# Streamed second attention: queries earlier and outputs later on TensorE, value halves first on ScalarE and VectorE, one turned load a store earlier

## The reference

```python
def _L1_xattn_ref(text_hidden, vision_tokens, vision_mask, Wq, Wk, Wv, Wo):
    q = (text_hidden @ Wq).reshape(B, T_text, N_HEADS, HEAD_DIM).transpose(0, 2, 1, 3)
    k = (vision_tokens @ Wk).reshape(B, T_vis, N_KV_HEADS, HEAD_DIM).transpose(0, 2, 1, 3)
    v = (vision_tokens @ Wv).reshape(B, T_vis, N_KV_HEADS, HEAD_DIM).transpose(0, 2, 1, 3)
    k = jnp.repeat(k, GROUPS, axis=1)
    v = jnp.repeat(v, GROUPS, axis=1)
    scores = jnp.einsum('bhtd,bhsd->bhts', q, k) / scale
    scores = jnp.where(mask, scores, -jnp.inf)
    attn = jax.nn.softmax(scores, axis=-1)
    out = jnp.einsum('bhts,bhsd->bhtd', attn, v)
    return out.transpose(0, 2, 1, 3).reshape(B, T_text, N_HEADS * HEAD_DIM) @ Wo
...
x = x + _L1_xattn_ref(_layernorm(x, axis=-1), ctx_1024, mask_BxS2_bf1, L1_xattn_Wq, L1_xattn_Wk, L1_xattn_Wv, L1_xattn_Wo)
```

## Time and profile before

| | |
|---|---|
| median of 3 runs | 2336.04 us |
| the profiled execution's own time | 2327.82 us |
| its span | 2326.0 us, mean granted clock 0.971 |
| PE busy | 2193.5 us (94%), 10153 matmuls |
| DVE, ACT, POOL busy | 1459.6 (63%), 1043.2 (45%), 771.1 us (33%) |
| streamed units | from about 885 to 1684 us |

### The profile page before, as it was taken

How to read it: one execution, slowest core, us unless ns; L and a number is a source line. 1 busy time by engine, 2 the same in 40 slices (tenths; PEclk the granted TensorE clock), 3 DMA queues, 4 the chain that set the end, 5 groups by cost and what they waited for, 6 DMA issues and landing times. The chain is left out here.

```text
span 2326.0 us, 32392 instructions
## 1 busy us (share of the span) xinstructions
PE 2193.5 (94%) x10153; PEld 1786.1 (77%) x10153; DVE 1459.6 (63%) x2989; ACT 1043.2 (45%) x1895; POOL 771.1 (33%) x705
## 2 busy tenths in 40 slices
PE   8999999999999997888888889888899999999999
PEld 6778788889999875666666666666677888888887
DVE  7755366647777676666666666666667555564544
ACT  5532211015565565556555556555555332332321
POOL 4423555511111443444444444444421302121000
PEclk9999999999999999999999999999999999999999
DMA  6423221127777766555555555555501223232331
GB/s 220 150 81 100 59 46 32 32 79 280 283 266 269 284 217 205 178 171 182 174 182 171 176 180 176 176 173 175 168 24 67 83 96 113 82 127 82 109 113 50
DMA packets 250573, 339.17 MB, mean 146 GB/s; under 512 B 22048, under 2 KB 159776, under 8 KB 247648
## 3 DMA queue, kind: packets, MB, share of 16 engines
q1 hardware_dynamic: 242224, 310.75, 40.7%
q0 software_dynamic: 8240, 27.01, 4.5%
HBM read 234.12 MB, written 103.55 MB: 145 GB/s over the span
## 5 line engine op out<-in xcount | busy, mean ns | idle before, releaser
L2269 POOL TENSOR_TENSOR xa_late_hi<-late_rows,route_wv_hi 128x512 fp32r<-128x512 f32 x228 | 290.3, 1295 | 389.5 <-ACT route_wv_hi L2336 388.6
L2362 ACT ACTIVATE route_weights<-route_weights,xa_minus_max 128x512 f32<-128x512 f32 x256 | 185.3, 724 | 360.8 <-DVE xa_minus_max L2562 360.7
L90 PE MATMUL xa_ps_o<-route_first_lo,xa_late_lo 128*128 128x512 f32 x256 | 114.3, 447 | 73.7 <-DVE xa_late_lo L2553 73.7
L2562 DVE CUSTOM_DVE_ANT_0 route_weights<-xa_ps_s,route_mask_bias 128x512 f32<-128x512 f32 x252 | 172.6, 685 | 9.8 <-issue 8.5
L2643 DVE STREAM_TRANSPOSE route_weights<-route_weights 128x512 f32<-128x512 f32 x228 | 160.0, 702 | 9.9 <-DMA xa_pt<-route_weights 7.4
L3305 ACT ACTIVATE ffn_silu<-ffn_ps_gate,late_scales 128x512 f32<-128x512 f32 x63 | 43.4, 688 | 247.3 <-PE ffn_ps_gate L92 247.3
L2584 DVE TENSOR_TENSOR x<-xa_ps_o,x 128x512 f32<-128x512 f32 x126 | 86.2, 684 | 92.1 <-PE xa_ps_o L92 92.0
L2336 ACT ACTIVATE route_wv_hi<-late_rows 128x512 fp32r<-128x512 f32 x228 | 129.6, 617 | 0.4 <-DMA late_rows<-xa_pt 0.4
L90 PEld LDWEIGHTS xa_ps_o<-route_first_lo,xa_late_lo 128*128 128x128 f32 x256 | 52.5, 205 | 96.4 <-issue 77.5
L90 PE MATMUL xa_ps_s<-route_kv_hi,xa_q_hi 128*128 128x512 f32 x256 | 110.8, 433 | 16.5 <-DVE xa_q_lo L2553 9.0
L1539 POOL DMA_INDIRECT route_rows<-moe_xn,route_slot_token x39 | 44.5, 1140 | 240.1 <-PE ex_ps_t L1832 182.5
(11 more groups left out here) (585 smaller groups left out, 6767.5 us busy)
## 6 DMA issues: line engine op xcount, KB each, us to landing
xa_pt<-route_weights SPq DMA_DIRECT2D x228, 256.0 KB, 2.0
late_rows<-xa_pt SPq DMA_DIRECT2D x456, 128.0 KB, 2.7
route_weights<-in_ffn_w SPq DMA_DIRECT2D x64, 512.0 KB, 3.7
route_weights<-in_expert_w SPq DMA_DIRECT2D x12, 1408.0 KB, 6.3
route_weights<-wd_folded SPq DMA_DIRECT2D x64, 256.0 KB, 2.6
ex_w_raw<-in_expert_w SPq DMA_DIRECT2D x10, 1408.0 KB, 6.3
moe_y<-ex_y SPq DMA_DIRECT2D x39, 256.0 KB, 3.6
route_weights<-in_expert_w SPq DMA_DIRECT2D x12, 768.0 KB, 8.9
```

The source lines that it names most:

```text
L90: pe.matmul(out, lh, rh, start=start, stop=False)
L2269: pool.tensor_tensor(lo, raw_part(half, two), f32(hi), ALU.subtract).then_inc(M.pt_ready, PART)
L2362: act.activation(prob[slot][:], prob[slot][:], ACT.Exp, bias=nmx[:, slot:slot + 1], scale=-1.0, accum_out=tot[:, slot:slot + 1]).then_inc( ...
L2562: dve.tensor_tensor_reduce(out=prob[slot][:], in0=psS[slot % 2][:], in1=mask_of(b, quarters), scale=-SCALE, scalar=3.4e38, op0=ALU.add, op ...
```

## The change

No operation is added, removed or resized. Four lists are put in another order. On PE the queries come right behind scores 3 and scores 0, the outputs behind scores 1 and scores 2. On ACT the value product's high half and the first turned half stand ahead of the first exponential, the second turned half behind it, the query's high half behind the exponential of tile 0, and the key or value copy later. On DVE the value product's low half comes right behind turn 0, the query's low half behind turn 3, and the additions to `x` around the last maximum. On SP the second half of a unit's turned tile is loaded behind its own store 3 instead of behind the next unit's store 0, and POOL makes all four low parts ahead of the key or value part. The order of waits moves with the operations.

```diff
--- before.py
+++ after.py
@@ -2216,21 +2216,19 @@
                     for ul, b, h, pair, u, i, left in units(g, which):
                         if which == "last" and ul > 0:
                             return
-                        before, again = features(g, which, ul, u)
 
                         def store(tt):
                             sp.wait_ge(M.blocks_turned, i + tt + 1)
                             sp.dma_start(G.pt_dram[ul % 2, tt], blocked[tt % 2][:]).then_inc(pt_stored[tt % 2], 16)
 
                         store(0)
-                        if before:
-                            load_turned((ul - 1) % 2, u - 1, 1)
                         store(1)
                         store(2)
                         if which == "first" and u == 0:
                             sp.wait_ge(R.xn_turned, NT)
                         load_turned(ul % 2, u, 0)
                         store(3)
+                        load_turned(ul % 2, u, 1)
                         if h == 1:
                             next_kv(pair + 1, g, b + 1)
                         if ul == 3:
@@ -2240,7 +2238,6 @@
 
                 groups(sp, body)
                 END = (GROUPS - 1) * UNITS + 1
-                load_turned(0, END - 1, 1)
                 load_gate_up(sp, io, G, L, 0)
                 load_down(sp, G, L, 0)
                 next_kv((GROUPS - 1) * B + 1, GROUPS - 1, 1)
@@ -2293,15 +2290,12 @@
                             break
                         before, _ = features(g, which, ul, u)
                         if before:
-                            turned_low(u - 1, 0, 0)
-                            turned_low(u - 1, 0, 1)
+                            for part in range(4):
+                                turned_low(u - 1, part // 2, part % 2)
                         if h == 0:
                             key_low(pair + 1, (b + 1) % B)
                         else:
                             kv_low(pair + 1, (b + 1) % B)
-                        if before:
-                            turned_low(u - 1, 1, 0)
-                            turned_low(u - 1, 1, 1)
                     if which != "last":
                         return
                     for part in range(4):
@@ -2419,24 +2413,24 @@
                         if which == "last" and ul > 0:
                             return
                         before, has_pv = features(g, which, ul, u)
-                        exp(i + 3, 3)
                         if has_pv:
                             proj_high(streamed_pv(u - 2), o_hi[out_buf((b - 1) % B if h == 0 else b - 1, h)])
                         if before:
                             turned_half(u - 1, 0)
+                        exp(i + 3, 3)
+                        if before:
+                            turned_half(u - 1, 1)
+                        normalise(halves(g, ul, 3), 3)
                         exp(i + 4, 0)
-                        normalise(halves(g, ul, 3), 3)
+                        proj_high(streamed_q(u), qh[h])
+                        exp(i + 5, 1)
                         loads = g * (B // 2) + (b + 1) // 2 + 1
                         if h == 0:
                             key_high(loads, (b + 1) % B)
                         else:
                             kv_high(loads, (b + 1) % B)
-                        exp(i + 5, 1)
-                        if before:
-                            turned_half(u - 1, 1)
+                        normalise(halves(g, ul, 5), 1)
                         exp(i + 6, 2)
-                        normalise(halves(g, ul, 5), 1)
-                        proj_high(streamed_q(u), qh[h])
                         if ul == UNITS - 3:
                             act.wait_ge(M.proj_done, streamed_q(u - 1).n + 1)
                             split_q(g + 1, 0)
@@ -2656,29 +2650,29 @@
                                 if n % STAGES < len(blocked):
                                     stored(dve, n)
                         turn_blocks(u, i, ul, 0, halves(g, ul, 0), before)
+                        if has_pv:
+                            o = out_buf((b - 1) % B if h == 0 else b - 1, h)
+                            proj_low(streamed_pv(u - 2), o_hi[o], o_lo[o])
                         masked_max(i + 3, 3, b)
                         if last:
                             dve.wait_ge(M.max_ready, i + 4)
                             for other in range(1, B):
                                 quarter_mask(maskb[:, (other - 1) * S:other * S], other)
                         normalise(i + 2, 2, halves(g, ul, 2))
-                        if has_pv:
-                            o = out_buf((b - 1) % B if h == 0 else b - 1, h)
-                            proj_low(streamed_pv(u - 2), o_hi[o], o_lo[o])
                         turn_blocks(u, i, ul, 1, halves(g, ul, 1), before)
                         masked_max(i + 4, 0, nb, last)
                         invert(i + 3, 3).then_inc(M.inv_ready, 1)
-                        if has_output:
-                            add_x(pair - 2 + h, (b - 2 + h) % B, 2 - 2 * h)
                         turn_blocks(u, i, ul, 2, halves(g, ul, 2), before)
                         masked_max(i + 5, 1, nb, last)
                         normalise(i + 4, 0, halves(g, ul, 4))
+                        turn_blocks(u, i, ul, 3, halves(g, ul, 3), before)
+                        proj_low(streamed_q(u), qh[h], ql[h])
+                        invert(i + 5, 1).then_inc(M.inv_ready, 1)
+                        if has_output:
+                            add_x(pair - 2 + h, (b - 2 + h) % B, 2 - 2 * h)
+                        masked_max(i + 6, 2, nb, last)
                         if has_output:
                             add_x(pair - 2 + h, (b - 2 + h) % B, 3 - 2 * h)
-                        turn_blocks(u, i, ul, 3, halves(g, ul, 3), before)
-                        masked_max(i + 6, 2, nb, last)
-                        invert(i + 5, 1).then_inc(M.inv_ready, 1)
-                        proj_low(streamed_q(u), qh[h], ql[h])
                         if ul == UNITS - 3:
                             split_q(g + 1, 0)
                         if ul == UNITS - 2:
@@ -2910,20 +2904,6 @@
                         nq = streamed_q(u)
 
                         scores(i + 3, 3, h, b % 2)
-
-                        if before:
-                            pe.wait_ge(M.proj_ready, streamed_q(u - 1).n + 1)
-                        if h == 1:
-                            pe.wait_ge(M.key_ready, pair + 2)
-                        scores(i + 4, 0, 1 - h, nk, last)
-                        if has_output:
-                            if ul == 3:
-                                pe.wait_ge(M.wo_ready, g + 2)
-                            if h == 1:
-                                pe.wait_ge(M.proj_ready, streamed_pv(u - 2).n + 1)
-                            output(pair - 2 + h, (b - 2 + h) % B, 2 - 2 * h)
-
-                        scores(i + 5, 1, 1 - h, nk, last)
                         if ul >= UNITS - HPG:
                             pe.wait_ge(M.q_ready, g * HPG + HPG + h + 1)
                         if which == "first" and ul == 0:
@@ -2933,11 +2913,25 @@
                             pe.wait_ge(M.proj_ready, streamed_q(0).n + 1)
                         bank_free(nq)
                         query(nq, qb, h, range(0, KC // 2))
+
+                        if before:
+                            pe.wait_ge(M.proj_ready, streamed_q(u - 1).n + 1)
+                        if h == 1:
+                            pe.wait_ge(M.key_ready, pair + 2)
+                        scores(i + 4, 0, 1 - h, nk, last)
+                        query(nq, qb, h, range(KC // 2, KC))
+
+                        scores(i + 5, 1, 1 - h, nk, last)
+                        if has_output:
+                            if ul == 3:
+                                pe.wait_ge(M.wo_ready, g + 2)
+                            if h == 1:
+                                pe.wait_ge(M.proj_ready, streamed_pv(u - 2).n + 1)
+                            output(pair - 2 + h, (b - 2 + h) % B, 2 - 2 * h)
+
+                        scores(i + 6, 2, 1 - h, nk, last)
                         if has_output:
                             output(pair - 2 + h, (b - 2 + h) % B, 3 - 2 * h)
-
-                        scores(i + 6, 2, 1 - h, nk, last)
-                        query(nq, qb, h, range(KC // 2, KC))
                         if before:
                             streamed_weighted(u - 1, pair - 1 if h == 0 else pair, (b if h == 1 else b - 1) % 2)
```

## The result

The changed kernel takes 2272.23 us (median of three, 2271.05 to 2273.13) against 2336.04: ratio 0.9726, interval 0.9704 to 0.9748, 63.8 us less. The forecast was 2209, with a range from 2182 to 2259. The direction held; half of the gain came, and the time lies outside the range. The profiled execution took 2273.13, span 2271.1, mean granted clock 0.985 (0.971 before).

What follows compares the result with a forecast made beforehand. It took TensorE's order-caused waits for the value product's low half, and low clock, as the bound. Seven groups at 92.4 us make 647 against 774, 127 less: 2327.8 to 2200.4, plus 8.2 carried, 2209 us; range 2182 to 2259.

Steps and rivals of the forecast that it cites:

- The two loops through the DMAs: Turn 3 to next turn 3 through store, loads and copies: 10.65 us behind even heads, 11.33 behind odd.
- What bounds the kernel: Streamed stretch: TensorE waits 72.0 us for the value product's low half, a wait of order, plus low clock behind it.
- Queries first: Queries wait for the next group's weight split in a group's last two units: 0.9 us, then near nothing; 1.0 per group.
- the 9.8: Assumed start, in us from a unit's first score matmul, of VectorE's last maximum, ahead of the weight split.
- Outputs last but one: Outputs end at 6.4 and 8.5 us of a unit, VectorE's additions run at 8 to 10.5: covered.
- Loads one store sooner: Second-half load behind its own store 3 makes SP wait 2.0 us for the landing; with the weight load, 91.4 a group.
- No instruction is added or removed; all costs are of order: Claim opening the part-by-part pricing: the change only reorders operations, so every cost comes from order.
- The lock: Rival: every VectorE scaling meets a whole GpSimd subtraction, 1.8 us per pair, 50 us: 2259 us; chance 0.07.
- the stall moves: Rival: ScalarE's second-half copy comes late, TensorE waits in every second unit's value product: 2295 us; chance 0.12.
- SP's queue turns the sign: Rival: slow landings on SP hold the next stores, 32.7 us a pair, 141 us more: 2477 us; chance 0.03.
- TensorE alone: Rival: nothing collides and the loops run under TensorE's 11.1 us a unit, 153 us less: 2183 us; chance 0.12.
- what would show it: Signs listed: stretch clock near 1.00, even units, loads 2.1 us behind store 3, about 1 us pause before seventh unit's queries.

Runs made afterwards that it cites:

- e9: The kernel before with only the value product's halves put first, on ScalarE and VectorE; loads and TensorE's order old: 2203.05 us, ratio 0.9455.
- e12: e9 with the second-half load also moved behind the unit's own store 3: 2303.20 us, ratio 0.9881.
- e4: The kernel before with only the second-half load moved behind the unit's own store 3: 2380.36 us, ratio 1.0201.
- e13: The changed kernel with the second-half load back behind the next store 0 and ScalarE's copy of it behind tile 1's exponential: 2277.50 us, ratio 0.9756.
- e17: e13 with ScalarE's key and value copy and GpSimd's key or value part back in their old places: 2212.42 us, ratio 0.9492.

## Why the prediction was right in part

The wait that the change removes was read rightly, and the gain of that part with it. Two steps of the working failed. The two loops through the DMAs were put at 10.65 and 11.33 us, no longer than TensorE's own work, and ran longer at every turn; and the move of the key and value parts was put at nothing.

**What bounds the kernel: right.** The wait for `xa_late_lo` was one of order, and e9, which changes only that order, takes it from 72.0 us to 9.3 and the stretch's clock from 0.93 to 1.00. 128 us came from it. That this equals the forecast's 127 for the whole change is a coincidence: the 127 rest on loops that e9, with its load in the old place, doesn't have.

**Queries first: the place right, the price wrong.** In the changed kernel the queries of the group's seventh unit wait for the weight split; the second of the two units runs at 11.11, as foreseen. But the wait is 3.0 us instead of 0.9, and not "short enough to leave the clock". The chain, on VectorE and then TensorE:

```profile
1164.12 0.68 DVE L2556 CUSTOM_DVE_ANT_0 route_weights<-xa_ps_s,route_mask_bias 128x512 f32<-128x512 f32 x1
...
1166.20 0.69 DVE L2538 TENSOR_TENSOR late_wq_lo<-route_weights,late_wq_hi 128x512 fp32r<-128x512 f32 x1 [0.80 <-ACT late_wq_hi L2344]
```

```profile
1167.03 0.79 PE L90 MATMUL xa_ps_p<-late_xT_hi,late_wq_hi 128*128 128x512 f32 x1 [3.03 <-DVE late_wq_lo L2538]
1167.62 0.63 PE L91 MATMUL xa_ps_p<-late_xT_lo,late_wq_hi 128*128 128x512 f32 x1
1168.04 0.63 PE L92 MATMUL xa_ps_p<-late_xT_hi,late_wq_lo 128*128 128x512 f32 x1
```

From the last maximum to the query are 2.9 us, as in the working (9.8 to 12.6). What failed is the 9.8: the maximum starts 13.3 us into its unit (1150.82 to 1164.12), since VectorE had stood 4.77 us in front of turn 2 one unit earlier and 1.27 in front of the next one (1159.24). The slack was counted against an undelayed VectorE. The matmuls then start 0.43 apart, and the unit takes 17.20 instead of 12.0, 5.2 more. I had priced the delays one by one; they add on one engine.

**Outputs last but one: covered, right.** In the stretch TensorE waits in front of no output.

**Loads one store sooner: the step that failed most.** Four things in it were wrong. The landing of store 3 was put at 2.05; the load follows 2.65 later in the rows above and 2.75 in those of e12 (medians of the stretch: 2.8 and 2.7). The rest of SP's row held: loads to keys 1.98 (1.95 forecast), keys to weights 2.64 (2.67). Second, the working has one weight load in a group and the kernel two: the output weights at the group's end got no term. From turn 3 to the next turn 3, read off VectorE's timeline and averaged over seven groups, pass 15.5 us there, where the loop of 11.33 was forecast; across the query weights 15.4, where it was 14.7; behind the other odd heads 12.3 (11.33); behind even heads 12.0 (10.65). A group is 103.5 by this against 91.4. The forgotten load is 4.1 of the 12.1, an estimate from these distances; no run moved it. And with loops of 10.65 and 11.33 against TensorE's 11.1 nothing was left for such an error, yet I forecast as if that balance were a gain. Last, I asked only what the longer loop would cost against TensorE's pace, not what the move does by itself: it costs 45 us in the kernel before (e4) and 100 in e9 (e12).

The traces tell when a store is late (900 to 1560, medians). In the kernel before, a store 3 issued less than 0.4 us behind the first half's loads landed in 2.76 us (14 of them), any other in 2.02 (33); the 2.0 of the earlier trace rows is the median of both kinds. In e9 all 55 follow that closely and take 2.67. With the load moved, the distance to the load is 2.68 behind the 15 close stores of e4 and 2.07 behind its 30 others, 2.91 (36) and 2.51 (15) in the changed kernel. One of e4's others, whose store comes 1.2 us behind the loads:

```profile
1106.06 0.34 SPq L2223 DMA_DIRECT2D xa_pt<-route_weights  x1
1108.12 1.78 SPq L2213 DMA_DIRECT2D late_rows<-xa_pt  x4
```

In the denser orders the store comes right behind the loads, and such stores land later; no run varied that distance alone. The Trainium skill, "DMA: Bandwidth & Descriptors", section on the anatomy of one DMA, gives 2.6 us by estimate for a 256 KB store, from a fit of DMAs that GpSimd issues. These are SP's, and the measured 2.02 of a store that stands free lies below it, the 2.67 and 2.76 of a close one just above; the measurements decide.

**"No instruction is added or removed; all costs are of order": a term is missing.** Key and value copy later on ScalarE, and POOL's four low parts ahead of the key or value part, got no sentence and no price; the section on the change speaks of four lists, but its diff has five, and GpSimd's is the one left out. They are the largest step of the ladder behind the first, 65 us (e13 against e17), through a wait on SP that the kernel before shows nowhere. `next_kv` on SP waits for that low part; I followed the queue's landings, and not its wait for GpSimd. In the changed kernel itself SP has no wait for GpSimd either: there SP comes later to `next_kv`, held by the landing of store 3. So the 65 us are shown with the load in its old place, and what the two parts cost in the changed kernel stays open.

**The lock: seen, not priced apart.** All scalings of the changed kernel, to hold against the earlier trace rows:

```profile
L2567 DVE TENSOR_SCALAR route_weights<-route_weights,xa_inverse x112: 485/782/1320, 889.6 to 1606.7; 128x512 f32<-128x512 f32 x112
```

The median went from 487 ns to 782. VectorE is busy 530 us of the stretch, in e9, where the median is 489 again, 509: some 20 us on an engine that others wait for. That GpSimd's subtractions are what stretches the scalings is argued, as it was ahead of the result. Which part of the 63 us it makes was not tried.

**The rivals.** What came is nearest to "the stall moves": the late turn 2 makes TensorE pause elsewhere, in scores and queries in the changed kernel (2272), in the value product in e12 (2303) and e4, where 2295 had been worked out. "SP's queue turns the sign" is right in its place: e4 is slower than before by it. TensorE alone (2183) was not reached by any version.

**Of what would show it**, the clock of the stretch (0.97, near 1.00 foreseen), the second-half load's distance (2.1 foreseen, 2.65), the units' evenness and the pause before queries (1 foreseen, 3.0) all spoke against the forecast's size; the vanished wait and the pause after the fifth unit's late store spoke for its mechanism.

Still open: the changed kernel with only its key and value parts put back was not tried, nor one with the output weights' load elsewhere, nor were the moved load's landing and its hold on store 0 told apart on their own.

## What to carry to other kernels

Where one order swap ends the wait that bounds the kernel, time that swap alone before the rest of a reordering: here it was worth 128 us, and the other moves took back 69. Before an operation is moved, list everything that waits for it on every queue, DMA queues too, and what stands behind that wait; here two moves on engines that are half idle cost 65 us (e13 against e17) through SP, which issues the DMAs. When a loop through a queue is added up, list every DMA that the queue issues in it, the rare ones too, and take a landing from rows with the same DMAs right in front of it. A slack counts against the start of the late engine, not against the pace of the bound one, and delays on one engine add.

## What was not expected of the hardware

The same pause lowered the clock once and left it once. In the changed kernel the wait for `late_wq_lo` in the group before is also 3.03 us, in TensorE's timeline:

```profile
1065.46 0.50 PE L90 MATMUL xa_ps_p<-late_xT_hi,late_wq_hi 128*128 128x512 f32 x1 [3.03 <-DVE late_wq_lo L2538]
1065.80 0.40 PE L91 MATMUL xa_ps_p<-late_xT_lo,late_wq_hi 128*128 128x512 f32 x1
1066.04 0.39 PE L92 MATMUL xa_ps_p<-late_xT_hi,late_wq_lo 128*128 128x512 f32 x1
```

Behind it the matmuls start 0.23 us apart, the level of 2.4 GHz; behind the one at 1167.03 they start 0.43 apart, that of 1.2 GHz. The windows behind the two, 1065.46 to 1078.93 and 1167.03 to 1180.50, have clocks of 1.00 and 0.77. So a pause of that length has no single price; two such stretches here differ by 0.2 us on each of the following dozen matmuls.
